# Eight PSUM banks dealt anew: one bank for value products, three for everything else, in an attention and mixture-of-experts kernel

## What is computed

```python
q, k, v = split_heads(x @ wq.T) * s, split_heads(x @ wk.T) * s, split_heads(x @ wv.T)
q, k = rope(q), rope(k)
attn = softmax(einsum("bhtd,bhld->bhtl", q, k) + causal_mask)
out = einsum("bhtl,bhld->bhtd", attn, v)             # heads joined again: (4, 2048, 256)
x1 = layernorm(x + out @ wo.T)
ri = concatenate([x1, stats(x1)], -1)                # mean, std, min, max, norm, share of zeros
h = gelu(ri @ r1_w.T + r1_b)                         # the hidden product of the router
```

## Time and profile before

| | us |
|---|---|
| median of three runs | 2455.76 (2455.72 to 2457.96) |
| the profiled execution, its own time | 2457.98 |
| its span, first to last instruction | 2456.2 |
| attention: start of the first exponential to start of the last hidden copy | 63.6 to 1645.0 |
| PE busy over the span | 1947.4 (79%) |
| mean granted TensorE clock | 0.892 of 2.4 GHz |

### The profile page before, as it was taken

The page is one execution under the profiler, slowest core; times in us unless marked ns, Lnnn a source line. Parts: engine busy times, 40 slices in busy tenths (PEclk is TensorE's granted clock), DMA queues, the critical chain, the costliest instruction groups (busy, mean ns, idle before and its releaser), DMA issues. The chain is left out here.

```text
span 2456.2 us, 36993 instructions
## 1 busy us (share of the span) xinstructions
PE 1947.4 (79%) x10914; PEld 1436.4 (58%) x10914; DVE 1562.3 (64%) x3363; ACT 1151.7 (47%) x2709; POOL 1372.6 (56%) x1723
## 2 busy tenths in 40 slices
PE   5899888888888888888888888845227999999990
PEld 3555555555555555555555555425126999999990
DVE  7565666665666666666666668637686666666655
ACT  3344345344444434434444444522525666666655
POOL 3368557556656755755665664420018566666653
PEclk7799999899999998999999999855558999999995
DMA  2000001011001101000011101122001444455428
GB/s 71 7 11 18 18 31 35 29 33 33 22 27 33 37 29 33 29 18 31 31 33 33 33 16 40 50 70 91 1 0 42 133 139 150 149 156 152 142 67 274
DMA packets 100610, 144.06 MB, mean 59 GB/s; under 512 B 17956, under 2 KB 88592, under 8 KB 96364
## 3 DMA queue, kind: packets, MB, share of 16 engines
q1 hardware_dynamic: 84588, 132.04, 15.7%
q0 software_dynamic: 15872, 10.24, 2.5%
HBM read 113.14 MB, written 39.85 MB: 62 GB/s over the span
## 5 line engine op out<-in xcount | busy, mean ns | idle before, releaser
L660 ACT ACTIVATE probs<-scores_t_ps 128x512 f32<-128x512 f32 (+3 forms) x640 | 338.0, 532 | 522.5 <-PE scores_t_ps L531 300.1
L782 DVE TENSOR_REDUCE part_max<-scores_ps 128x1 f32<-128x512 f32 (+3 forms) x640 | 373.3, 601 | 190.7 <-PE scores_ps L511 104.1
L511 PE MATMUL scores_ps<-k_st,q_two 128*128 128x512 f32 (+3 forms) x640 | 279.1, 453 | 61.4 <-DVE part_max L782 46.0
L357 POOL TENSOR_TENSOR sums<-sums,probs 128x512 f32<-128x512 f32 (+3 forms) x288 | 321.5, 1116 | 10.3 <-ACT probs L660 5.7
L1555 PE MATMUL up_ps<-xe_t,w 128*128 128x320 f32 x1920 | 289.6, 311 | 1.7 <-DVE xe_t L1662 1.7
L547 PE MATMUL out_ps<-probs,v_sb 128*64 128x512 f32 (+3 forms) x1280 | 290.5, 578 | 0.0
L1555 PEld LDWEIGHTS up_ps<-xe_t,w 128*128 128x128 f32 x1920 | 284.8, 189 | 2.0 <-issue 1.9
L530 PE MATMUL scores_t_ps<-q_two,k_st 128*128 128x512 f32 (+3 forms) x640 | 274.2, 428 | 5.9 <-ACT probs L660 5.9
L444 PE MATMUL proj_ps<-w_qkv,x_t_parts 128*128 128x384 f32 x696 | 172.7, 390 | 91.9 <-DVE k_st L752 88.4
L531 PE MATMUL scores_t_ps<-q_low,k_one 65*128 65x512 f32 (+3 forms) x640 | 242.3, 379 | 0.0
L357 DVE TENSOR_TENSOR sums<-sums,probs 128x512 f32<-128x512 f32 (+3 forms) x288 | 226.8, 787 | 7.4 <-ACT probs L660 3.8
(11 more groups left out here) (257 smaller groups left out, 3805.0 us busy)
## 6 DMA issues: line engine op xcount, KB each, us to landing
w_raw<-in_w_expert SPq DMA_DIRECT2D x32, 1536.0 KB, 6.5
x_t<-in_x_t SPq DMA_DIRECT2D x128, 128.0 KB, 2.0
w_raw<-in_w_adapter SPq DMA_DIRECT2D x32, 384.0 KB, 7.2
x_row<-in_x SPq DMA_DIRECT2D x64, 128.0 KB, 2.0
x_rows<-x SPq DMA_DIRECT2D x64, 128.0 KB, 2.0
acc_rows<-x SPq DMA_DIRECT2D x64, 128.0 KB, 2.0
ln_x<-acc_rows SPq DMA_DIRECT2D x16, 512.0 KB, 6.1
out_rows_dram<-ln_y SPq DMA_DIRECT2D x16, 512.0 KB, 5.1
```

The source lines that it names most:

```text
L357: eng.tensor_tensor(side, side, probs[:, g % P_RING, i * P:CH], ALU.add).then_inc(summed[u % 2], 1)
L511: mm = pe.matmul(out[:, 0:n], q_two[:, ring, hh, cols(i)], k_st[:, hh, places(f * NT + 4 * c, 4)][:, 0:n], start=True, stop=not diagonal)
L660: act.activation(probs[:, g % P_RING, i * P:CH], s_ps[:, g % 2, i * P:CH], ACT.Exp).then_inc(exp_done, 1)
L782: dve.tensor_reduce(part_max[:, u % 4, i, c:c + 1], x_ps[:, e % 2, 0:n], AX.X, ALU.max).then_inc(score_read, 1)
```

## The change

`Plan` deals three banks, a, b and c, by a list. `claim(kind, k, at)` looks for the first slot from `at` on in which some bank has no use in that slot, the one before or the one after, and takes the bank whose last use is oldest. Steps are dealt in this order: proj and kt, then sum and spread (spread at least two slots after sum), then wo, x1t and hidden, then qt. Projections keep their base slots; keys keep base + 6. wo, x1t and hidden get distances of at least 2, 7 and 1 from one another instead of fixed ones. The value products have one bank; a new ACT step `out`, late in the slot that begins the next group, copies them to `attn` once the group's value products are done, and PE's first value product of a group waits for that copy. `norm` on ACT is gone; DVE's `norm` multiplies the spread bank with that copy. `stats` on DVE and POOL is split: the row's maximum and all after it move to `stats2`, one slot later. The hidden product waits for `x1_split` by itself.

```diff
-        base_of, used = {}, set()
+        self.bank = {("qt", n): "abc"[n % 3] for n in range(8)}
+        last_use, uses = {"a": -9, "b": -9, "c": -9}, set()
+
+        def claim(kind, k, at):
+
+            while True:
+                open_banks = [b for b in "abc" if not any((b, s) in uses for s in (at - 1, at, at + 1))]
+                if open_banks:
+                    bank = min(open_banks, key=lambda b: last_use[b])
+                    last_use[bank] = at
+                    uses.add((bank, at))
+                    self.bank[kind, k] = bank
+                    return at
+                at += 1
...
-            base_of[n] = base
-            used |= {("a", base), ("a", base + 6)}
...
+            at = base_of[n] = claim("proj", n, max(base, at))
+            back = keys_at[n] = claim("kt", n, max(at + 6, back))
...
-            sum_at.append(free("a", begin[y + 1] + 1))
-            spread_at.append(free("a", sum_at[y] + 1))
...
+            sum_at.append(claim("sum", y, max(begin[y + 1] + 1, at)))
+            at = claim("spread", y, sum_at[y] + 2)
+            spread_at.append(at)
...
-                at = max(at + pace if post else 0, spread_at[y] + 1)
-                post.append(at)
-        slots = self.slots = post[-1] + 14
+                at = max(at + pace if m else 0, spread_at[y] + 1)
+                out_at = claim("wo", m, max(at + 2, out_at + 4))
+                turn_at = claim("x1t", m, max(out_at + 7, turn_at + 2))
+                if m % 2:
+                    hidden_at = claim("hidden", m, max(turn_at + 1, hidden_at))
+                post.append((out_at, turn_at, hidden_at if m % 2 else turn_at + 1))
...
+            late[begin[y + 1]].append(("out", y))
...
-                    while ("a", at) in used and ("b", at) in used:
-                        at += 1
-                    self.q_bank[n] = "b" if ("a", at) in used else "a"
-                    used.add((self.q_bank[n], at))
+                    at = before = claim("qt", n, max(at, base_of.get(n, -10) + 5, before))
...
+        for m, (at, turn, last) in enumerate(post):
+            early[at - 1].append(("ot_read", m))
+            late[at].append(("wo", m))
+            early[at + 1].append(("wo_read", m))
+            early[at + 1].append(("ln", m))
+            early[at + 2].append(("x1", m))
+            late[at + 3].append(("stats", m))
+            late[at + 4].append(("stats2", m))
+            late[turn].append(("x1t", m))
+            early[turn + 1].append(("x1t_read", m))
+            late[last].append(("hidden", m))
+            early[last + 1].append(("hidden_read", m))
...
-        o_ps = ctx.enter_context(nc.psum_tensor("out_ps", [P, 2, CH], F32))
-        a_ps = ctx.enter_context(nc.psum_tensor("proj_ps", [P, CH], F32))
-        b_ps = ctx.enter_context(nc.psum_tensor("misc_ps", [P, CH], F32))
+        o_ps = ctx.enter_context(nc.psum_tensor("out_ps", [P, CH], F32))
+        misc = {b: ctx.enter_context(nc.psum_tensor(f"misc_{b}_ps", [P, CH], F32)) for b in "abc"}
...
-                        at_least(pe, attn_ready, u // 2 - 1)
-                    mm = pe.matmul(o_ps[hh * HD:(hh + 1) * HD, u // 2 % 2, i * P:CH], v_sb[:, place(f * NT + kb), hh, :],
+                        at_least(pe, out_copied, u // 2)
+                    mm = pe.matmul(o_ps[hh * HD:(hh + 1) * HD, i * P:CH], v_sb[:, place(f * NT + kb), hh, :],
...
-                    claim("a", spread_copied, k + 1)
+                    out = claim(kind, k, attn_ready, k + 1)
...
-                    claim("b", hid_copied, k // 2 + 1)
-                    out = b_ps[:, D:2 * D]
+                    out = claim(kind, k, hid_copied, k // 2 + 1)[:, D:2 * D]
+                    pe.wait_ge(x1_split, k + 1)
...
-                elif kind == "norm":
+                elif kind == "out":
                     f, G = groups[k]
-                    act.wait_ge(spread_done, k + 1)
+                    act.wait_ge(values_done, begin[k + 1] // BATCH)
                     act.wait_ge(weights_split, 8)
                     at_least(act, attn_split, NT * (f // 2 - 1) + 4 * G + 4)
-                    act.copy(attn[:, f % 2, G * CH:(G + 1) * CH], a_ps[:]).then_inc(spread_copied, 1)
+                    act.copy(attn[:, f % 2, G * CH:(G + 1) * CH], o_ps[:]).then_inc(out_copied, 1)
...
-                    dve.wait_ge(spread_copied, k + 1)
-                    dve.wait_ge(values_done, begin[k + 1] // BATCH)
+                    dve.wait_ge(spread_done, k + 1)
+                    dve.wait_ge(out_copied, k + 1)
                     out = attn[:, f % 2, G * CH:(G + 1) * CH]
-                    dve.tensor_tensor(out, o_ps[:, r, :], out, ALU.mult).then_inc(attn_ready, 1)
+                    dve.tensor_tensor(out, bank("spread", k)[:], out, ALU.mult).then_inc(attn_ready, 1)
...
                     dve.tensor_reduce(x1[:, r, D + 2:D + 3], row, AX.X, ALU.min)
+                elif kind == "stats2":
+                    row = x1[:, r, 0:D]
                     dve.tensor_reduce(x1[:, r, D + 3:D + 4], row, AX.X, ALU.max)
```

More of the change, by code:

```diff
@@ L85, in __init__ @@
         per = total // PH
-        base_of, used = {}, set()
+        self.bank = {("qt", n): "abc"[n % 3] for n in range(8)}
[10 more added lines that the diff above has]
+                at += 1
+        base_of, keys_at = {}, {}
+        at = back = 0
         for n in range(FIRST, self.PROJ):
@@ L132, in __init__ @@
             early[base + 1].append(("proj_read", n))
-            late[base + 6].append(("kt", n))
-            early[base + 7].append(("kt_read", n))
-            turned[n] = base + 7
+            late[keys_at[n]].append(("kt", n))
+            early[keys_at[n] + 1].append(("kt_read", n))
+            turned[n] = keys_at[n] + 1
         entries, cur = [], total
@@ L144, in __init__ @@
         entries.reverse()
-        q_from, self.q_bank = [], {n: "ab"[n % 2] for n in range(8)}
+        q_from, before = [], 0
         for y, (f, G) in enumerate(self.groups):
@@ L357, in add_up, with bank @@
                 eng.tensor_tensor(side, side, probs[:, g % P_RING, i * P:CH], ALU.add).then_inc(summed[u % 2], 1)
-        def q_bank(n):
-            return (a_ps if plan.q_bank[n] == "a" else b_ps)[:, 0:D]
+        def bank(kind, k):
+            return misc[plan.bank[kind, k]]
         def walk(main, step, score, ahead):
@@ L480, in _, with claim @@
             pending = {}
[L482 to L486, removed]
+            def claim(kind, k, semaphore, value):
+                name = plan.bank[kind, k]
+                if name in pending:
+                    pe.wait_ge(*pending[name])
+                pending[name] = semaphore, value
+                return misc[name]
             keys_seen, ones_seen, values_seen = [0], [0], [0]
@@ L590, in step @@
                 elif kind == "wo":
-                    claim("b", resid_done, k + 1)
+                    out = claim(kind, k, resid_done, k + 1)
                     pe.wait_ge(attn_split, k + 1)
@@ L595, in step @@
                     for c in range(2):
-                        mm = three(b_ps[:, 0:D], lambda a: attn_t[:, a, c, :], lambda b: w_o[:, b, c, :],
+                        mm = three(out[:, 0:D], lambda a: attn_t[:, a, c, :], lambda b: w_o[:, b, c, :],
                                    start=c == 0, stop=c == 1)
@@ L680, in step @@
                 elif kind == "proj_read":
-                    copy_qkv(a_ps, k)
+                    copy_qkv(bank("proj", k), k)
                 elif kind == "kt_read":
-                    upper_k(a_ps[:, 0:D], k)
+                    upper_k(bank("kt", k)[:, 0:D], k)
                 elif kind == "qt_read":
@@ L720, in step @@
                     side = k % 2
-                    act.copy(x1_t[:, 0, :, side], b_ps[:, 0:D].rearrange("p (a b) -> p a b", b=P))
-                    act.copy(x1_ts[:, 0, side], b_ps[0:NSTAT, D:D + P]).then_inc(x1_upper, 1)
+                    act.copy(x1_t[:, 0, :, side], bank("x1t", k)[:, 0:D].rearrange("p (a b) -> p a b", b=P))
+                    act.copy(x1_ts[:, 0, side], bank("x1t", k)[0:NSTAT, D:D + P]).then_inc(x1_upper, 1)
                 elif kind == "hidden_read" and k % 2:
@@ L726, in step @@
                     at_least(act, hid_stored, 32 * j)
-                    act.copy(hidden[:].rearrange("p a b -> p (a b)"), b_ps[:, D:2 * D]).then_inc(hid_copied, 1)
+                    act.copy(hidden[:].rearrange("p a b -> p (a b)"), bank("hidden", k)[:, D:2 * D]).then_inc(hid_copied, 1)
             walk(main, step, score, exp)
@@ L801, in step @@
                 if kind == "kt_read":
-                    lower_k(a_ps[:, 0:D], k)
+                    lower_k(bank("kt", k)[:, 0:D], k)
                 elif kind == "qt_read":
@@ L818, in step @@
                     dve.wait_ge(totals_ready, k + 1)
-                    dve.reciprocal(inverse[:], a_ps[0:8, 0:P]).then_inc(totals_read, 1)
+                    dve.reciprocal(inverse[:], bank("sum", k)[0:8, 0:P]).then_inc(totals_read, 1)
```

(4 more changed lines are left out.)

58 lines of the change are left out of this document (21 added, 37 removed).

## The result

The changed kernel takes **2303.05 us** (median of four runs, 2294.73 to 2305.46); the kernel before 2456.86 beside it. The ratio is 0.9367, 95% interval 0.9341 to 0.9393.

What follows compares the result with a forecast made beforehand. The prediction took PE's waits for a PSUM bank to bound the attention part. Waits 98, norm 2, statistics 1, clock 8 and tail 1 summed to 110 us, from 2457.98 to 2348 us, range 2305 to 2412.

Steps and rivals of the forecast that it cites:

- The clock term: PE's short stretches at 1.2 GHz in the middle: some go with fewer bank waits, 8 us, bounds 0 and 51.
- the removed waits: PE's 127.8 us of waits for a bank in the attention part go; 98 us gained, bounds 80 and 128.
- norm and statistics: DVE's multiplication no longer waits for ACT's spread copy, 2 us; part_max can pass between the split router statistics, 1 us.
- tail: After the last exponential, ACT's copy between last spread and DVE's multiplication goes: 1 us gained, bounds 0 and 4.
- What bounds the kernel: The attention part is PE's; its idle time can be won, mostly waits for a bank DVE has not yet read.
- the refill: Part of the removed waits not gained because PE comes earlier to its next wait for DVE or ACT.
- Query turns up to three slots later: Attention part: some scores bunch and may wait for part_max, 0 to 6 us of loss, taken as 0.
- The sign that I had set for this: Granted clock of the middle going over 0.97 would show that the clock term was too small.
- One value bank: At group ends, PE's wait for ACT's copy is covered by three slots of work: 0, at most 18 us late.
- The clock rival: All 127.8 us of bank waits and half the low clock's price go: 157 us, about 2301, chance 0.11.

Runs made afterwards that it cites:

- The wait put back: Changed kernel, with projections sharing a slot with a turn of keys again waiting until DVE has read those keys (50 places): 2430.48 us, ratio 0.9903.
- the one with two banks: Changed kernel with its list dealing only banks a and b, neighbouring slots allowed, the eighth bank idle: 2344.09 us, ratio 0.9537.
- The kernel with whole statistics: Changed kernel with the router statistics in one slot again instead of split over two: 2293.67 us, ratio 0.9346.

## Why the prediction fell short

The cause was right and two terms of the sum were too small. The clock term, taken as 8 us, answers to 43.9 us less busy time, and the removed waits, taken as 98 us, to 115.2 us less idle time.

Term by term: idle time for bank waits 98, measured 115.2 in the three stretches (200.1 + 21.4 + 17.3 before; 93.1 + 13.8 + 16.7 after); clock 8, where PE's busy time fell by 37.5 + 4.2 + 2.2 = 43.9 (the last 80 slots also hold 11 matmuls fewer); norm and statistics 3, measured none; tail 1, measured -5.7. The sum of what was measured is 153.4; the span fell by 152.7.

- **What bounds the kernel: right.** PE's waits for the bank were the place. 88.4 and 27.2 us went; putting one wait back costs 127 us.
- **Removed waits, 98 us taken from bounds of 80 and 128: too small by 17.** All of the 127.8 us went but 3.6. PE's idle time fell by 7.6 us in the first 80 slots and by 107.0 in the middle. I had read the refill, the part that comes back in other waits, from calm stretches, 9.4% idle; after the change the middle is 93.1/1050.3 = 8.9% idle. The wait put back shows a refill of one sixth, where I had taken off a quarter.
- **Query turns up to three slots later, taken at 0 (bounds 0 to 6): wrong.** By the list 9 of the 120 turns come four or five slots later. Scores now wait 30.3 us for q_low, from 1.0; with the query turns in their old slots (three banks, neighbours allowed) it is 7.9. It is not a loss of 30, though: in the run with scores three slots later nearly all of it came back as other waits.
- **Clock, 8 us from bounds of 0 and 51: the step that failed.** The middle's time at 1.2 GHz, summed over the granted clock, fell from 133.1 to 78.5 us, 41% of it, where 8 of 51 us is 16%. The price was too low as well. Over the thirteen kernels with the same 5161 or 5162 recorded matmuls in the middle, PE's busy time rises by 0.49 us for each us at the low clock (from 934.5 us busy at 17.1 us low to 1003.1 at 153.6; all lie within 8 us of the line but the one with two banks, 18 above it). Fitted with the number of PE's stops beside it, it is 0.40 us, and 0.21 us a stop. The kernel before and the one with one value bank, with the same idle time, give 8.5 us busy for 20.5 us low, 0.41. So the clock makes 22 to 27 of the 37.5 us. I had priced one low us at 1 - 1/1.56 = 0.36, from mean durations, whose records overlap. The busy time in the same, 1.8 us for 4 products and 5.6 for 22, is 0.45 and 0.25 us a product, 1.77 times, and would have given 0.43. And I had let the last 80 slots (clock 0.93) speak for the changed middle. The sign that I had set for this, a clock over 0.97, did not come either: it was 0.96. The Trainium skill's rule that I set beside the term (TensorE: Matmul & The Clock Gate, A second HAM failure mode: psum-queue depth-cycling) would have made it 0. The runs go against that use of it: the kernel cycles through more banks than before for these steps, and its clock is higher, with fewer and shorter idle gaps.
- **Not in the sum: what a stop costs beyond its idle time.** The other 10 to 16 us of busy time go with 76 fewer stops of PE in the middle (235 to 159 gaps of over 30 ns between its records), 0.13 to 0.21 us each. My reading is that the recorded end of a matmul reaches over the next one's start, as in the time line above (the turn at 608.87 takes 0.38 us, the projection starts at 609.01), and before a stop there is no next one. This share is what the clock leaves, not measured by itself. Kernels with more stops have more low time too (correlation 0.6), so the two parts are divided only roughly, and the reading is argued, not shown.
- **Norm 2, statistics 1: 0.** Neither showed in the run of each alone.
- **One value bank at 0: right**, by itself 1.0011.
- **Tail 1 us: wrong sign**, 5.7 us longer. The sums start 3.9 us later, behind the router product that the list moved there, and take 1.6 us longer at the low clock; 0.6 us of ACT's copy are saved, and 0.8 are lost behind.
- **The rivals.** The clock rival (157 us, 2301, chance 0.11) named the mechanism that the forecast had too small. That its sum came so near is in part luck: it had 128 for the waits, where 115.2 came, 25 for the clock, where 43.9 came, and 4 for the rest, where the tail lost 5.7. The range ended at 2305, inside that rival's 2290 to 2325.

## What to carry to other kernels

When steps share a PSUM bank, look in the list of waits for a matmul that waits on the reader of another step's content; two steps dealt into one slot cost 1.67 us a time here, and dealing the steps over the two banks already there brought three quarters of the gain, before any third bank. Count such a wait at more than its recorded length where PE is the bound: here 1.3 times, since more of the time is at the low clock. Slack given to a wait is worth it only if it presses nothing else together: one slot for the router product gave 18 us (by the ratios 24), one for the scores cost 17 (10).

## What the runs showed of the hardware

DVE's busy time in the middle rose by 20.8 us (762.86 to 783.63) with the same work. Three of its lines in the middle by shape (count, busy, mean ns), before and after:

```profile
L782 DVE TENSOR_REDUCE part_max<-scores_ps 128x1 f32<-128x512 f32 x336 | 222.8, 679 | 87.1 <-PE scores_ps L511 85.5 <-issue 0.2
L357 DVE TENSOR_TENSOR sums<-sums,probs 128x512 f32<-128x512 f32 x144 | 128.4, 892 | 2.2
...
L822 DVE TENSOR_TENSOR attn_t<-attn,attn_t 128x256 fp32r<-128x256 f32 x48 | 32.9, 686 | 4.5 <-ACT attn_t L699 4.5
```

```profile
L796 DVE TENSOR_REDUCE part_max<-scores_ps 128x1 f32<-128x512 f32 x336 | 222.1, 677 | 41.4 <-PE scores_ps L526 38.5 <-issue 0.2
L370 DVE TENSOR_TENSOR sums<-sums,probs 128x512 f32<-128x512 f32 x144 | 156.8, 1089 | 1.3
L836 DVE TENSOR_TENSOR attn_t<-attn,attn_t 128x256 fp32r<-128x256 f32 x48 | 39.5, 824 | 23.7 <-ACT attn_t L713 23.5
```

The maxima, which read PSUM, kept their 679 ns (677 after). The additions went from 892 to 1089 ns and the subtractions for attn_t from 686 to 824: both read two tensors in SBUF, and POOL reads SBUF too. The Trainium skill has this as a rule (SBUF — State Buffer, Who interferes with whom): an instruction of DVE with two SBUF inputs contends with one of POOL that reads SBUF. The trace agrees: the additions with under 50 ns of a POOL instruction beside them took 682 ns on average in both kernels (44 of 144 before, 6 after), and POOL was at work during 71% of the additions' time before and 87% after.

It is not the pace alone that brings this. The kernel with whole statistics has as fast a middle, and POOL busy for the same 73% of it, but DVE has 759.13 us and the additions take 937 ns, with POOL at work during 81% of them:

```profile
241.40:1282.70 1041.30, 953.28 (x5163) 621.53 (x5162) 759.13 (x1729) 516.05 (x1393) 757.16 (x1056) 0.97 0.11 34
```

```profile
L370 DVE TENSOR_TENSOR sums<-sums,probs 128x512 f32<-128x512 f32 x144 | 135.0, 937 | 1.3
```

With the split and the old wait put back (middle 1174.70 us) DVE has 761.15. So the 20.8 us, which the sum had left out, come with the split of the statistics at the faster pace: it moves additions into times in which POOL works. It may be why the split, which was to let part_max pass, is worth nothing; no run shows that by itself.
